# A six-layer decoder on one core: squares and transposes of x taken batch by batch, and batch 0's products placed in front of the transposes of batches 2 and 3

## The reference

```python
norms = jnp.linalg.norm(x, axis=-1)
dots = jnp.einsum('bil,bjl->bij', x, x)
sim = dots / jnp.maximum(norms[:, :, None] * norms[:, None, :], EPS)
atten = jax.nn.softmax(sim, axis=-1)
out = jnp.einsum('bij,bjl->bil', atten, x) + x
```

## Time and profile before

| | us |
|---|---|
| median of 3 runs | 1117.17 |
| lowest and highest | 1117.06 and 1117.23 |
| profiled execution | 1118.83 |
| its span | 1117.10 |
| TensorE busy in the span | 1032.1 (92%) |
| VectorE busy | 733.3 (66%) |
| ScalarE busy | 503.9 (45%) |
| GpSimd busy | 248.7 (22%) |

### The profile page before, as it was taken

One profiled execution on the slowest core, in us unless ns is written; L12 is line 12 of the kernel. 1 busy time (PEld: TensorE's weight loads), 2 busy tenths in 40 slices (PEclk: granted clock), 3 DMA queues, 4 the chain that ended last, 5 costly groups with the idle time before them and its releaser, 6 DMA issues.

```text
span 1117.1 us, 18196 instructions
## 1 busy us (share of the span) xinstructions
PE 1032.1 (92%) x6782; PEld 880.4 (79%) x6782; DVE 733.3 (66%) x1724; ACT 503.9 (45%) x933; POOL 248.7 (22%) x308
## 2 busy tenths in 40 slices
PE   6859889999998599999999999999999999999884
PEld 3647678888886378999999999999999999999521
DVE  5876867655566668778767667658576657763236
ACT  4336554333235554544434444434444434543373
POOL 7111410054736222212121111112111111110001
PEclk9979999999999699999999999999999999999997
DMA  7100000000001000000000000000000000000001
GB/s 235 8 1 1 1 1 1 1 1 2 1 1 38 0 1 2 1 2 1 1 1 1 1 1 2 1 2 2 1 2 1 2 1 1 2 1 1 1 0 38
DMA packets 16130, 10.14 MB, mean 9 GB/s; under 512 B 9207, under 2 KB 15275, under 8 KB 15531
## 3 DMA queue, kind: packets, MB, share of 16 engines
q1 hardware_dynamic: 16043, 8.97, 2.8%
HBM read 7.61 MB, written 1.05 MB: 8 GB/s over the span
## 4 chain that ended last, share of the span: by engine, by line
PE 82%; DVE 9%; ACT 5%; issue 2%; DMA 1%; POOL 1%; POOLq 0%; ACTq 0%; DVEq 0%
PE PS L1481 79%; PE PS L1493 2%; PE PS L1852 1%; DVE st L1009 1%; DVE BIG L1103 1%; DVE mx L1100 1%; DVE KB L1313 1%; DVE X_EVEN L1020 1%; DVE X_ODD L1020 1%; ACT BIG L731 1%; ACT REG L971 1%; DVE mv L1012 0%; ACT BIG L761 0%; DMA QB<-crow 0%; ACT BIG L739 0%
## 5 line engine op out<-in xcount | busy, mean ns | idle before, releaser
L1481 PEld LDWEIGHTS PS<-VXA,BIG 128*128 128x128 f32 (+1 forms) x3136 | 400.4, 191 | 26.7
L1481 PE MATMUL PS<-VXA,BIG 128*128 128x65 f32 (+2 forms) x3136 | 395.4, 271 | 0.0
L945 ACT ACTIVATE BIG<-PS 128x512 f32<-128x512 f32 (+1 forms) x320 | 189.8, 593 | 228.5 <-PE PS L1481 227.8
L1369 DVE TENSOR_REDUCE mxm<-PS 128x1 f32<-128x512 f32 x256 | 170.7, 688 | 83.0 <-PE PS L1481 78.0
L1481 PE MATMUL PS<-QA,KA 128*128 128x512 f32 (+1 forms) x320 | 145.1, 454 | 0.3
L1481 PE MATMUL PS<-QB,KB 128*128 128x512 f32 (+1 forms) x320 | 125.9, 393 | 0.0
L1481 PE MATMUL PS<-KA,QA 128*128 128x512 f32 (+1 forms) x512 | 116.3, 331 | 0.9 <-POOL KA L677 0.6
L677 POOL CAST KA<-KA 64x78 fp32r<-64x78 f32 (+1 forms) x128 | 54.9, 429 | 220.9 <-ACT KA L918 217.3
L1481 PEld LDWEIGHTS PS<-KA,QA 128*128 128x128 f32 x512 | 87.4, 191 | 21.0 <-DVE mxm L1369 1.7
L918 ACT ACTIVATE KA<-PS,b1s 64x78 fp32r<-64x78 f32 (+1 forms) x128 | 64.3, 502 | 84.2 <-PE PS L1481 82.6
L677 POOL CAST QB<-QA 64x512 fp32r<-64x512 f32 x64 | 39.0, 609 | 257.4 <-ACT QA L918 257.2
(11 more groups left out here) (256 smaller groups left out, 1511.4 us busy)
## 6 DMA issues: line engine op xcount, KB each, us to landing
X_EVEN<-in_x SPq DMA_DIRECT2D x4, 256.0 KB, 3.9
VXA<-in_L_ffn_Wg SPq DMA_DIRECT2D x1, 1024.0 KB, 6.1
VXA<-in_L_ffn_Wu SPq DMA_DIRECT2D x1, 1024.0 KB, 8.0
VXA<-in_L_ffn_Wd SPq DMA_DIRECT2D x1, 1024.0 KB, 9.8
REG<-in_L_xattn_Wkv SPq DMA_DIRECT2D x1, 1024.0 KB, 4.9
QB<-crow SPq DMA_DIRECT2D x64, 2.0 KB
out<-X_EVEN SPq DMA_DIRECT2D x4, 256.0 KB, 2.3
wq1s<-in_L_xattn_Wq SPq DMA_DIRECT2D x1, 512.0 KB, 8.3
```

The lines of the kernel that those rows point to most:

```text
L945: act.activation(PX[0:rows, g % 4, :], PS[0:rows, g % 2, :], ACT.Exp, scale=SCALE_W).then_inc(pw_ready, 1)
L1369: dve.tensor_reduce(mxm[:, p % 2, h, m:m + 1], PS[:, 2 + g % 2, :], AX.X, ALU.max).then_inc(mu_free, 1)
L1481: return pe.matmul(dst, lhsT, rhs, start=start, stop=stop, **kw)
```

## The change

Three engines get another order in the first layer. What is computed is the same.

ScalarE squared all four batches and then copied the four transposes. Now it goes batch by batch: squares of batch 0, copy of `xT` 0, squares and copy of batch 1, the copy of `rb` 0, then squares and copy of batch 2, and of batch 3.

TensorE transposed all four batches first. Now `rb` and the dots of batch 0 stand behind the transposes of batch 1, and the transposes of batches 2 and 3 behind these dots. The product for the bias row `cb0` moves from `context0` to behind `out_a(0)`.

VectorE clamped the sums of all batches and then built all diagonals. Now the diagonal of batch 0 comes before the clamps of batches 2 and 3. Its addition for `CB0` moves behind `out_a(0)`.

The numbering of both lanes follows.

```diff
 def lane_a_tasks():
-    t = [("xT", "A", b) for b in range(B)] + [("rb", 0), ("ctxT",)] + [("rb", b) for b in range(1, B)]
+    t = [("xT", "A", 0), ("xT", "A", 1), ("rb", 0), ("xT", "A", 2), ("xT", "A", 3), ("ctxT",)] + [("rb", b) for b in range(1, B)]
 def lane_v_tasks():
-    t = [("k0",), ("v0",), ("cb0",)] + [("oA", b) for b in range(B)]
+    t = [("k0",), ("v0",), ("oA", 0), ("cb0",)] + [("oA", b) for b in range(1, B)]
...
-            for b in range(B):
+            def squares(b):
+
                 act.wait_ge(x_in[b], 16)
...
-            for b in range(B):
+
+            for b in range(2):
+                squares(b)
+                evac(("xT", "A", b), XT[:, b, :])
+            evac(("rb", 0), RBv[:, 0, :])
+            for b in range(2, B):
+                squares(b)
                 evac(("xT", "A", b), XT[:, b, :])
             for b in range(B):
-                evac(("rb", b), RBv[:, b, :])
+                if b:
+                    evac(("rb", b), RBv[:, b, :])
...
-            for b in range(B):
+            def sums(b):
+
                 dve.wait_ge(sq_ready, NT * (b + 1))
...
+            sums(0)
+            sums(1)
             for b in range(B):
+                if b == 1:
+                    sums(2)
+                    sums(3)
                 dve.wait_ge(rn_ready, b + 1)
...
                 out_a(b)
+                if b == 0:
+                    bias0()
...
-            for b in range(B):
+            def turn_x(b):
+
                 pe.wait_ge(x_in[b], 16)
                 lane_a(("xT", "A", b), transposes(tiles_of(xtile("0", b))))
+
+            turn_x(0)
+            turn_x(1)
...
             dots(0)
+            turn_x(2)
+            turn_x(3)
             context0()
             for b in range(B):
                 if b + 1 < B:
                     dots(b + 1)
                 out_a(b)
+                if b == 0:
+                    bias0()
```

More of the change, by code:

```diff
@@ L1075, in context0, with bias0 @@
                 dve.tensor_copy(v0x[:, :, :, 0:DH], bank_v(n)[0:CK, :].rearrange("p (b h d) -> p b h d", b=B, h=NH)).then_inc(v_free, 1)
+            def bias0():
                 n = LV["cb0",]
```

## The result

| | before | changed |
|---|---|---|
| median, us | 1117.17 | 1121.37 |
| lowest to highest | 1115.43 to 1118.04 (7 runs) | 1120.02 to 1122.25 (7 runs) |
| profiled execution | 1118.83 | 1121.64 |
| its span | 1117.10 | 1119.9 |

The changed kernel is slower: ratio 1.0037, 95% interval 1.0027 to 1.0046, that is 3.0 to 5.1 us. The forecast was 3.6 us.

What follows compares the result with a forecast made beforehand. TensorE was taken as 82% of the chain, with VectorE working nearly without a pause from 31.73 us. A loss of 4.2 us up to `out_a(0)` less 0.6 given back made +3.6, from 1117.17 to 1120.8 us; range 1118.8 to 1123.6.

Steps and rivals of the forecast that it cites:

- (a): TensorE, first layer: `rb` of batch 0 starts at 9.2 us instead of 12.64, a gain of 3.4 us there.
- (b): TensorE: batch 0's products run longer on the slow clock, which rises at 13.5; the dots end at 15.70 us.
- (c): ScalarE: squares of batch 3 fall behind TensorE's `dots(0)`; the last clamp comes at 18.11 against 10.19, 7.92 us late.
- (d): GpSimd's memset of `VBD` blocks the first scaling of `sims(0)`, costing 2.3 us; first similarity at 23.28 against 16.49.
- rival of the weak block: The memset of `VBD` hardly blocks VectorE's scaling: +1.6 us instead of +3.6, 1118.8; chance 0.14 including the clock's return.
- (e): To the end of `context0`: `sims(1)` can start at 30.56 against 25.28, 5.28 us late instead of 6.79.
- (f): VectorE's `out_a(0)`: 5.28 us late, old wait of 1.42 absorbed, 3.86 remain; `CB0` costs 0.33 more: +4.2 us.
- (g): Start of the cross attention: a sooner clock rise gives back at most 1.2 us, 0.6 taken.
- The clock pays for everything: Slow stretches at 61 to 75 and 375 to 385 us shorten: 5.3 us back against 4.2, 1116.1; chance 0.04.

## Why the prediction was right, point by point

The time was foreseen as 1120.8 and is 1121.37; sign, place and cause are those of the forecast. That the number is so close is luck in part. The span of the profiled execution was foreseen as 3.6 us longer and is 2.8 longer. But the forecast kept the 1.66 us by which the profiled execution of the kernel before stood above the median, and that of the changed kernel stands only 0.27 above its own; this adds 1.4 to the difference of the medians. The two misses, 0.8 too much and 1.4 too little, work against each other.

(a) *Batch 0 sooner.* `rb` 0 at 9.2 was 9.01; 0.14 of it is the first square, at 5.24 instead of 5.38. Right.

(b) *The clock.* A rise at 13.5 was assumed, 4.3 us behind `rb`. In the profiled runs it came before 12.6 (changed), between 14.3 and 15.1 (memset moved, and the squares ahead), with `rb` near 9.0 each time. The lag is not a constant; the mechanism was right and the size was a draw. The dots ended 0.5 sooner than in the sum.

(c) *Squares behind TensorE.* The last clamp at 18.11 was 17.59. Undoing this alone takes 6.9 us away, against 7.1 that the expectation had (1113.9 against 1121). This step is shown.

(d) *The long memset.* Expected: a scaling from 20.45 that ends at 23.26. Measured: 19.93 to 22.30. The whole-instruction wait was the right end of the range, and moving the memset removes it. The rival of the weak block is dead, but its 2.0 us were not found in the time. Without the squares in front the medians give 0.8: the way from the last clamp to the first similarity was shorter by the full 1.91 (2.84 against 4.75 us), but the clock rose later in that run and the clamp was 1.18 later. With them the medians give 1.6, and `out_a(0)` is 0.72 sooner, because VectorE then waited for TensorE. The row at 60.41 from which the forecast took the lock was a weaker witness than it seemed: the scaling there began before the addition that it waited for, so issue order alone does not explain it (see the last section).

(e) *`context0`.* `sims(1)` expected 5.28 us late, was 4.20 (29.48 against 25.28). Of the 1.08 between them, 0.52 come from the sooner dots of (b), 0.42 from a shorter way between the clamp and the end of the blocked scaling, and the rest from `sims(0)` and `context0`.

(f) *To `out_a(0)`.* Expected 3.86 late, was 3.42. Here a term was put at nothing: the later memsets were to cost nothing, and `sims(1)` was taken at its old pace, 4.9 us. It took 5.5 (29.48 to 34.95), with scalings of 0.81 us beside GpSimd's memsets of `KB`, which had moved there (30.54 to 34.83). The wait of 1.42 was absorbed as said. `CB0` cost 0.20 instead of 0.33 (38.44 to 38.64), so 3.62 in place of 4.2.

(g) *Given back.* 0.6 expected, 0.64 measured, by the profiled run. That was luck: with the memset moved the clock rose later, the products at 70.05 and 74.58 us both took 1.41, and 0.96 more was lost instead (14.68 us from the first maximum to the third product, against 13.72 before and 13.08 in the changed kernel). The bounds of this term, 0 to 1.2 given back, were too narrow.

The gain side had a term that the sum did not price as a gain. Moving the bias row is worth 2.2 us alone, and 6 us inside the changed kernel, where its absence lets TensorE stand for 9 us and the clock fall. The prediction had it as two waits that go; the right sum, but it does not show that everything else in the change costs some 10 us (1127.41 against 1117.48).

*The clock pays for everything* did not happen: the second long stretch moved with the work (between 385 and 390 us the granted clock was 0.70 in the changed kernel and 0.95 before), and the n-th product at 407 us is 0.2 us nearer, no more.

What stays open: the profiled runs put the slip at 2.8 us at the end and the medians at 4.2. The steps at 335 to 408 and 1027 to 1108 us are large enough for it, but unprofiled runs show no place, so this is argued, not shown.

## What to carry to other kernels

When a loop over batches on one engine is split so that the first batch can go ahead, look for the consumer that waits for all batches; here one wait for `sq_ready` of 16 tiles turned 3.6 us of head start into 5.8 us of delay, and two lines that put the squares first took the delay away. But that kernel was then only some 0.3 us ahead of the one with the moved bias row alone, a small part of the change, in the profiled runs. Run the parts alone before one of them gets the credit. Follow also what stands behind the late step on a side engine: a memset that cost nothing where it was made a scaling of VectorE 1.9 us longer where it landed. And judge such a change by where the difference is carried from, not by single runs: past that place, in the profiled runs, it moved only where the clock fell and rose.

## What the runs showed of the hardware

- A VectorE instruction between tiles in SBUF can wait for a whole GpSimd instruction. A cast of 8 columns took 2.43 us beside a memset of 2.50 us, and 0.17 without it. The Trainium skill, page "SBUF — State Buffer", section "Who interferes with whom", describes this as an exclusive lock for a full instruction, for VectorE in its two-port modes, and the length of the wait agrees with it.
- The power on GpSimd did not do this: four scalings took 1.10 us beside it (55.96 to 57.06, the power from 56.13). In the earlier trace rows the scaling at 60.41 began 0.91 us before the addition that is seen to block it, while the power was still running, and with that addition moved away the block was gone. So by the recorded times the block set in before the blocking instruction began. Why was not tried.
- After `rb` 0 had begun near 9.0 us, the lower clock lasted at most 3.6 us in one profiled run (the load at 12.59) and at least 5.2 us in two others (a load of 0.34 at 14.24 in the run with the squares, at 14.31 with the memset moved), with the same instructions on TensorE up to there.
- A wait of 9.05 us on TensorE cost 2.1 us more behind it, 0.9 in one product and 1.2 in the four dots, since they ran on the lower clock (granted 0.50 from 29 to 34 us).
- Idle products kept the clock up in a wait of TensorE: behind eight of them (7.13 us) and behind eleven (9.71 us) the first score products took 0.80 us instead of 1.41.
